# Attention's max subtraction for five of eight steps: from TensorE in PSUM to VectorE, with the exponential in place in SBUF

## What is computed

```python
q = q * jax.lax.rsqrt(jnp.linalg.norm(q, axis=1, keepdims=True) + EPS)   # k likewise
dots = jnp.einsum('bhid,bhjd->bhij', q, k)
scores = jax.nn.softmax(dots / scale[:, None, None], axis=-1)
out = jnp.einsum('bhij,bhjd->bhid', scores, v)
...
h = _layernorm(h + attn(h))
h = _layernorm(h + ffn(h))
```

## Time and profile before

| | us |
|---|---|
| median of 3 runs | 136.16 (135.83 to 136.19) |
| profiled execution, its own time | 136.0 |
| its span in the trace | 134.2 |
| busy in the span: PE, PEld | 127.7, 119.3 |
| busy in the span: DVE, ACT, POOL | 95.5, 81.3, 74.7 |
| attention's steps (from the first scores to the last transposition) | about 39 to 70 |

### The profile page before, as it was taken

How to read it: one execution, slowest core, us unless ns; L and a number is a source line. 1 busy time by engine, 2 the same in 40 slices (tenths; PEclk the granted TensorE clock), 3 DMA queues, 4 the chain that set the end, 5 groups by cost and what they waited for, 6 DMA issues and landing times. The chain is left out here.

```text
span 134.2 us, 3973 instructions
## 1 busy us (share of the span) xinstructions
PE 127.7 (95%) x1564; PEld 119.3 (89%) x1565; DVE 95.5 (71%) x240; ACT 81.3 (61%) x168; POOL 74.7 (56%) x83
## 2 busy tenths in 40 slices
PE   6999999999999999999999999999999999999960
PEld 2778999999899999999989999999899999999950
DVE  0009689927967969567677688898987776788862
ACT  3028689998865258487759673655354446333771
POOL 7300428953078999998760482689853442344600
PEclk9999999999999999999999999999999999999996
DMA  4899974550022222522393047600006650000022
GB/s 129 272 384 405 412 265 158 154 210 0 5 66 56 66 57 70 150 70 76 89 330 126 0 94 171 164 26 0 0 0 156 146 144 20 5 2 0 2 67 65
DMA packets 8987, 15.47 MB, mean 115 GB/s; under 512 B 1224, under 2 KB 5896, under 8 KB 8968
## 3 DMA queue, kind: packets, MB, share of 16 engines
q1 hardware_dynamic: 8968, 15.22, 36.5%
HBM read 9.96 MB, written 0.44 MB: 78 GB/s over the span
## 5 line engine op out<-in xcount | busy, mean ns | idle before, releaser
L542 POOL TENSOR_TENSOR reg_r<-reg_p,reg_r 128x324 fp32r<-128x324 f32 (+1 forms) x23 | 18.7, 811 | 19.2 <-ACT reg_r L793 19.1
L482 POOL TENSOR_TENSOR reg_w<-stage,reg_w 128x768 fp32r<-128x768 f32 x12 | 22.3, 1867 | 10.9 <-DVE w L1121 6.3
L793 ACT ACTIVATE reg_r<-reg_p 128x324 fp32r<-128x324 f32 (+1 forms) x23 | 10.2, 444 | 13.5 <-DVE reg_p L1172 13.4
L1377 PE MATMUL ps<-reg_r,reg_w 128*128 128x324 f32 (+1 forms) x48 | 15.0, 312 | 0.0
L784 ACT ACTIVATE ps<-ps,sm 128x252 f32<-128x252 f32 (+1 forms) x21 | 9.7, 464 | 8.7 <-PE ps L1381 8.5
L1380 PE MATMUL ps<-reg_r,reg_w 128*128 128x324 f32 (+1 forms) x48 | 14.2, 296 | 0.0
L1378 PE MATMUL ps<-reg_r,reg_w 128*128 128x324 f32 (+1 forms) x48 | 14.2, 295 | 0.0
L1381 PE MATMUL ps<-reg_r,reg_w 128*128 128x324 f32 (+1 forms) x48 | 14.1, 295 | 0.0
L1379 PE MATMUL ps<-reg_r,reg_w 128*128 128x324 f32 (+1 forms) x48 | 14.1, 294 | 0.0
L1137 DVE TENSOR_SCALAR ps<-ps,bup 128x252 f32<-128x252 f32 (+1 forms) x21 | 10.8, 513 | 3.3 <-PE ps L1381 3.2
L518 POOL TENSOR_TENSOR reg_q<-reg_q,rnorm 128x432 f32<-128x432 f32 x7 | 8.9, 1275 | 6.4 <-ACT rnorm L679 6.4
(11 more groups left out here) (206 smaller groups left out, 391.2 us busy)
## 6 DMA issues: line engine op xcount, KB each, us to landing
reg_x<-xw_in SPq DMA_DIRECT2D x5, 416.0 KB, 6.6
stage<-w_gu_a SPq DMA_DIRECT2D x4, 384.0 KB, 3.6
stage<-w_gu_b SPq DMA_DIRECT2D x4, 384.0 KB, 4.0
reg_r<-reg_x SPq DMA_DIRECT2D x24, 54.0 KB
stage<-w_qkv_a SPq DMA_DIRECT2D x3, 384.0 KB, 8.1
stage<-w_qkv_b SPq DMA_DIRECT2D x3, 384.0 KB, 8.0
stage<-w_down SPq DMA_DIRECT2D x3, 384.0 KB, 3.8
stage<-wrow SPq DMA_DIRECT2D x8, 126.0 KB, 2.4
```

Source lines behind the costliest of these rows:

```text
L482: nc.gpsimd.tensor_tensor(dst[:, 1, :], raw, f(dst[:, 0, :]), ALU.subtract).then_inc(s_wlop, 1)
L542: nc.gpsimd.tensor_tensor(acts[:, n % NACT, 1, 0:w], act_f[:, n % 4, 0:w], f(acts[:, n % NACT, 0, 0:w]), ALU.subtract).then_inc(s_alo, 1)
L793: nc.scalar.activation(acts[:, n % NACT, 0, 0:w], act_f[:, n % 4, 0:w], ACT.Copy).then_inc(s_ahi, 1)
L1377: mm(out_ap, w_a(0), x[:, 0, cols], start=True, stop=False)
```

## The change

For steps 3 to 7 the two matmuls of `subtract_max` go away. VectorE runs a `tensor_tensor` in their place right behind `row_max(u)`, which adds the negated maximum to the scores from PSUM and writes into the probabilities' slot in SBUF. ScalarE's exponential then reads and writes that slot. The last matmul of `scores(u)` carries the stop flag instead.

```diff
+SUB_DVE = 3
@@ exps(u), ScalarE
                 act.wait_ge(s_sub, u + 1)
                 if u >= 3:
                     act.wait_ge(s_pt, u - 2)
+                if u >= SUB_DVE:
+                    nc.scalar.activation(slots_of(u, slice(0, LANES)), slots_of(u, slice(0, LANES)), ACT.Exp).then_inc(s_e, 1)
+                    return
@@ VectorE
+            def subtract_max(u):
+
+                dve.wait_ge(s_mx, u + 1)
+                dve.wait_ge(s_pt, u - 2)
+                b = s_bank(u)
+                nc.vector.tensor_tensor(slots_of(u, slice(0, LANES)).rearrange("p (b h) j -> p b h j", b=2),
+                                        ps[0:LANES, b:b + 2, 0:6 * SEQ].rearrange("p b (h j) -> p b h j", h=6),
+                                        f(mx_r[0:LANES, u % 2, :]).rearrange("p (b h) -> p b h", b=2).unsqueeze(3)
+                                        .to_broadcast([LANES, 2, 6, SEQ]), ALU.add).then_inc(s_sub, 1)
@@ VectorE's loop
                 if k + 1 < NU:
                     row_max(k + 1)
+                if SUB_DVE <= k + 1 < NU:
+                    subtract_max(k + 1)
                 if k == 6:
                     ln1(1)
                 row_recip(k)
@@ TensorE's loop
             for k in range(2, NU - 1):
-                subtract_max(k)
+                if k < SUB_DVE:
+                    subtract_max(k)
                 scores(k + 1)
...
-            subtract_max(7)
             h1_transpose(0)
```

More of the change, by code:

```diff
@@ L1488, in scores @@
                             last = mm(ps[64 * img:64 * img + n, bank + b, c:c + SEQ], qk[rows, m, t:t + n],
-                                      qk[rows, NP + m, t:t + SEQ], start=(i == 0 and r == 0), stop=False,
+                                      qk[rows, NP + m, t:t + SEQ], start=(i == 0 and r == 0),
+                                      stop=(u >= SUB_DVE and i == 2 and r == 1),
                                       skip_group_check=True)
```

## The result

The changed kernel takes 138.65 us (median of 4 executions, 137.97 to 139.81) against 136.18 for the kernel before beside it: ratio 1.018, 95% interval 1.013 to 1.023. It is slower. The profiled execution is the slowest of the four, 139.81 us with a span of 138.0, and it holds two things that have to be taken apart: a shift that every execution has, and one episode at half clock that only some have.

The account below looks back on a forecast made before the run. TensorE and the chain through VectorE and GpSimd's full queue were taken to bound the kernel nearly together. Delays of 0.65 + 0.65 + 0.65 = 1.95 us on the median 136.16 gave 138.1, range 136.2 to 138.8.

Parts of the forecast that it names:

- The addition, 0.60: On VectorE, each 432-element addition takes 0.60 us (bounds 0.49 and 0.75); what stands behind a row_max comes 0.65 later.
- What the change takes away, 1.68: On TensorE, the five removed subtractions save 0.28 or 0.42 us each, 1.68 in all, 1.40 of it ahead of project(2).
- Step 1: Attention step 3's addition, ahead of step 2's reciprocal, moves probs(2) 0.65 us later; TensorE's first 0.56 saving is lost.
- Step 2: Attention step 4's addition: q_norm(6) starts 0.65 us later, meets the same two GpSimd instructions and ends 0.65 later.
- rival (a): q_norm(6) gets in at the first GpSimd boundary, the end of w_lo(7); project(2) 1.15 us later, 137.3; chance 0.22.
- Step 3: Attention step 5's addition, ahead of step 4's reciprocal, adds 0.65 us; project(1) 1.30 later, TensorE waits some 1.5.
- Step 4: After project(1): attention step 6's addition costs nothing, step 7's ahead of ln1(1) adds 0.65 us; project(2) 1.95 later.
- Step 5: Behind project(2): no list is changed and TensorE stays busy, so the 1.95 us is carried to the end.
- Rival (d): TensorE's clock falls to half in one of the two new waits; 1 to 2 us more, 139 to 140; chance 0.06.
- (b): Both ln1 come before TensorE asks, so the removed subtractions count in full: faster, 134.5 us; chance 0.09.
- (c): q_norm(6) misses GpSimd's instructions altogether: nearly no change, 135.8 to 136.5 us; chance 0.08, 0.05 for just above.

Follow-up runs that it names:

- e1: The changed kernel with its five additions moved behind ln1(1) and the reciprocal, still ahead of q_norm; 137.21 us, ratio 1.0076.
- e7: e1 with GpSimd's list reordered: k_norm(7) and root(0) ahead of w_lo(8), later w_lo behind the probs of their steps; 136.78 us, ratio 1.0041.
- e9: The changed kernel with additions behind q_norm (attention steps 3, 5), ahead of q_norm(6) (4), behind ln1(1) and the reciprocal (6, 7); 135.91 us, ratio 0.9997.
- e10: e9 with GpSimd's reordered list of e7; 135.53 us, ratio 0.9956.
- e5: The kernel before with only attention step 3 subtracted on VectorE; 136.37 us, ratio 1.0013.
- e6: The kernel before with only attention steps 4 and 6 subtracted on VectorE; 135.50 us, ratio 0.9957.
- e2: The kernel before with only attention step 7 subtracted on VectorE; 136.16 us, ratio 1.0015.
- the repetition: The changed kernel measured once more, with nothing altered, against the kernel before; 139.17 us, ratio 1.0191.
- e12: The kernel before plus one small VectorE write to a spare tile, behind the reciprocal of attention step 5; 135.75 us, ratio 0.9965.
- e3: The kernel before with only attention step 5 subtracted on VectorE; 136.46 us, ratio 1.0037.

## Why the prediction was right, step by step

**The addition, 0.60, and 0.65 for what stands behind it.** Right: 0.607. The Trainium skill ("VectorE: DVE Perf Modes", the section on the SBUF errata) gave an estimate of 0.575; the line through the two rows was nearer for this order. In e1, e7, e9 and e10, where other instructions stand between `row_max` and the addition, it took 0.577 to 0.587 on average, which is nearer to the page. The exponential in place takes 0.556 to 0.565 and is hidden.

**What the change takes away, 1.68.** This term was too large. The prediction took the distance from a subtraction's start to the next block. But without the pair the next block also starts later behind the one ahead of it. `scores(6)` start 2.46 behind `project(0)` before and 2.26 in the changed kernel:

```profile
54.05 0.38 PE L1547 MATMUL ps<-ident,hb 128*108 128x128 f32 x2
...
56.51 0.83 PE L1488 MATMUL ps<-reg_q 64*64 64x36 f32 x45
```

```profile
54.54 0.38 PE L1564 MATMUL ps<-ident,hb 128*108 128x128 f32 x2
...
56.80 0.83 PE L1504 MATMUL ps<-reg_q 64*64 64x36 f32 x45
```

So that subtraction was worth 0.20, not 0.42. Read in the same way the other four are worth 0.19 to 0.20 each, about 1.0 us in all. And all five stand ahead of `project(2)` in TensorE's list, not 1.40 of 1.68. It did no harm to the forecast, because the forecast lets all of it be lost. The wait of "some 1.5" ahead of `project(1)` came out partly by luck: it is counted from 58.6 without taking the 0.42 off, by which it would have been 1.9; TensorE was ready only 0.17 sooner, and the wait was 1.51.

**Step 1.** Right: `probs(2)` +0.63 (0.65 forecast), and TensorE waits 0.38 for `probs(3)` at the transpositions of step 3, which start at 14.00 from the first `row_max`, within 0.05 of where they were (53.49 - 39.54 = 13.95). What the first two subtractions had saved is lost there; it was 0.40 (the weighted sums ahead of it start at 12.70 instead of 13.10), not 0.56.

**Step 2.** Right for the place: `q_norm(6)` starts 0.65 later and is 2.47 long. So rival (a) is out here. Why it is so is told by e5, e6 and e9: the end hangs on the end of `probs(3)` in every case. The distance from `w_lo(7)`, by which the prediction argued, doesn't decide it: `q_norm(6)` starts 0.05 after it in e5, 0.69 in the changed kernel, 1.19 in e9 and 1.29 in e6, and does not get in at that boundary in any of them. Why the one at 45.63 did get in at the first boundary was not shown. The Trainium skill ("SBUF — State Buffer", section "Who interferes with whom") has the second to start blocked until the first has finished. No kernel here shows that at `q_norm(6)`; the earlier trace rows at 45.63 does.

**Step 3.** Right: `probs(4)` +1.27, `root(0)` +1.28 (from the first `row_max` 17.81 to 19.09), `project(1)` +1.28, TensorE idle 1.51 ahead of it; forecast 1.30 and some 1.5.

**Step 4.** Right: step 7's addition ahead of `ln1(1)` costs 0.57 more, `project(2)` +1.85 against 1.95 forecast. Of the 0.10 too much, 0.02 is left over from `project(1)`, and 0.08 lies ahead of the addition: `ln1(1)` follows the addition by 0.53 and ends at 66.03, and `project(2)` follows by 0.15 as before, but from `project(1)` to `row_max(7)` the list takes 3.58 us (60.57 to 64.15) instead of 3.66 (58.82 to 62.48). e2 alone shows 0.64 for the same edit, so the addition's own price is the forecast one.

**Step 5, the shift carried to the end.** Right in size, +1.80, and not constant: 0.36 is given back in the experts and 0.31 lost again near the end, both by a gap in VectorE's list that moved. By that, an execution without a half-clock episode should take 136.18 + 1.80 = 137.98; those measured are 137.45 to 138.05.

**Rival (d), the clock, chance 0.06.** Undersized, and it is the one thing that put the median above the forecast. The prediction let the clock fall inside one of the waits. It is at 1.00 in both. In the profile it falls 6 us later, in a stretch of short transpositions and weighted sums, and costs 1.57; 6 of 10 executions have a mean clock that low or lower. The median of four, 138.65, is the middle of two executions without it and two with it; no execution is near 138.65. That this median lies inside the range is partly luck: the repetition's, 139.17, would lie outside it. Whether the waits are behind it is not shown. By the mean clock there are two kinds of fall, one like the profiled (0.979 to 0.985) and a longer one (0.96, in e12's profile 10 us). The first kind came in 5 of the changed kernel's 10 executions, in 7 of 70 of the kernel before, and in none of 6 with the waits filled, which speaks for the waits; but six executions are few. e3, with a wait of 0.89, had it in 3 of 10, and e1, with one of 1.42, in none of 4. The longer kind came in 1 of 10, 3 of 70 and 1 of 6, and in e12's profile, with no wait added, it begins at the same place of TensorE's list. So the place is not made by the waits; at most they make the short fall there more frequent.

**Rivals (b) and (c).** Out in this order of the list. e9 and e10 show what they asked for, an addition that delays nobody. Then the time is that of (c), no change to 0.4% faster, and not (b)'s 134.5. That number took off 1.68 where the starts give about 1.0, and between the projections the round of statistics, root and layer norm (4.69 and 4.96 us in e10) covers most of the rest.

## What to carry to other kernels

Before work is moved to an engine that is less busy, ask what stands behind the new instruction in that engine's list and who waits for it. Here 0.6 us in front of a reciprocal and of a layer norm delayed TensorE by 0.6 us each, with VectorE busy for 71% of the span; the same instruction behind them, and not directly ahead of a `q_norm`, cost nothing. Taking about 1.0 us from the busiest engine was worth almost nothing, since each projection waits for a chain through other engines that the projection before it starts. And what an instruction is worth is read from the distance between the blocks around it, with and without it, not from its own start to the next. And when a change moves the time by 0.3%, test it against a change that only adds an empty instruction.

## What the runs showed that was not expected

- A VectorE `tensor_tensor` with both inputs in SBUF keeps a GpSimd instruction out while it still stands queued behind another that doesn't: `probs` took 1.71 and 1.72 us instead of 1.15 in e1 and e7, 1.15 again when `q_norm` stood first, and 0.91 beside an addition with no `q_norm` behind it.
- The same `tensor_tensor`, once waiting, did not get in at the end of the first GpSimd instruction in any kernel here, only behind the second: 1.87 to 3.11 us long, with its end about 0.46 behind `probs(3)`.
- An addition that reads PSUM and SBUF runs beside GpSimd at no price to either (0.59 and 1.15).
- A gap of 0.44 to 0.46 us in VectorE, with nothing waited for, moves or goes with the number of instructions ahead of it. One instruction of 0.06 us took 0.3% (0.1 to 0.6%) off the run.
- TensorE's clock fell to half for 3.4 us while TensorE was busy with short matmuls, 6 us behind the last wait. In the one profile of a kernel without added waits that holds a fall (e12, 10 us long), it begins at the same place of the list.
